# A decoder layer on one core: the expert stage's second bias as one float32r product of split rows

## The chip, the cores and the metric

The kernel runs on one core of one Trainium2 chip. Its time is the device time of one execution in microseconds (us). A core has TensorE (matrix products; loads of its stationary operand are listed apart), VectorE, ScalarE and GpSimd (in the rows: PE, PEld, DVE, ACT, POOL), and a queue for transfers on SyncE (SP). They run side by side, each through its own list of instructions, and wait for one another on semaphores. Products go into eight banks of PSUM, everything else on the core lies in SBUF.

## The reference, cut to what matters

A decoder layer for x of 16 x 128 x 256: self attention, cross attention, and a third block with an attention of its own and four experts. Only the last part is touched, on 2048 tokens with 4 experts and 256 hidden columns:

```python
raw = softmax(x @ w_gate)                    # 4 values for each token
top_vals, top_idx = top_k(raw, 2)
w = softmax(top_vals)
comb = zeros((t, 4)).at[arange(t)[:, None], top_idx].add(w)
hmid = gelu(einsum('td,edi->tei', x, we1) + be1[None])
eout = einsum('tei,eid->ted', hmid, we2) + be2[None]
out = einsum('te,ted->td', comb, eout)       # then h + out and a layer norm
```

The bias be2 enters as comb @ be2: for each token the sum of four rows of be2, each times its gate weight.

## The kernel before, in words

The program runs its stages one after another on each engine: A and B (the first two attentions), C (the third), D (the experts). The order of the work in each engine's list is written out by hand. Stage D takes the 2048 tokens as 16 blocks of 128, in four chunks c of four blocks b; experts are x = 0 to 3. Chunk 0's hidden layer is made at the end of stage C. Then for c = 1 to 3 a loop over m = 0 to 7 makes the hidden layer of chunk c (one half of one expert for each m) and, at each odd m, combines one block of chunk c-1. Chunk 3 is combined last, by itself.

float32 values are multiplied exactly enough by splitting them: a high part rounded to float32r, and a low part that is the value minus the high part. A product of split values is three products (high x high, high x low, low x high), and float32r products of 256 columns are one pass each. In stage D:

- hidden_pe (L2066) makes a half of an expert's hidden layer in six products (L2074 to L2076). hidden_act (L2254) applies gelu (L2263) and rounds to the high part D_HH (L2269), hidden_pool (L2302) subtracts to get the low part D_HL (L2305). xt_pe, xt_act, xt_low turn the normalized x of a later chunk and split it in the same way (L1621 is the subtraction).
- gate_pe (L2053) makes the gate's logits with 4 columns each (L2062); gate_dve, in three parts, makes the gate weights in some eighteen small instructions on VectorE (L2142 to L2183). The last writes 16 values for each token, 4 blocks x 4 experts, into the first 16 columns of D_comb, a 128x128 tile that is otherwise zero.
- comb_t_pe (L2079) transposes D_comb on TensorE (L2082), so that the weight of block b and expert x lies in row 4b+x, and comb_t_act (L2271) copies the 128x128 result from the bank to D_combT on ScalarE (L2275).
- TensorE's combine (L2093) makes, for each block, six products for each expert (L2115 to L2117) and one for the bias (L2109), ahead of expert 1's, or of expert 2's in the last chunk. The bias product has D_combT as stationary operand and one block of the table D_b2, 128x4x256, as moving one: rows 4b to 4b+3 of block b hold be2, the others are zero. Both are plain float32. An expert's bank is used again four turns later, when VectorE has read it.
- VectorE's combine (L2188) waits for the first expert's bank with the bias, adds the residual to the bias (L2196), adds the four experts times their gate weight one after another (L2202) and takes the statistics for the layer norm (L761 to L765). GpSimd raises the variance to the power -0.5 (L771), and VectorE's finish applies it to the block before (L776). In the last chunk ScalarE scales experts 0 and 1 (L2299), GpSimd sums them with the residual (L2341, L2344), and VectorE does the bias (L2214) and experts 2 and 3 (L2221).
- norm_step (L1565 to L1578) and norm_pool (L1584) normalize the blocks of a later chunk for its hidden layer; VectorE does two steps at each m below 4 in c = 1 and 2.
- SyncE loads the table once (L2366), when stage C is nearly over, and stores each block when it is done.
- The turns of banks 6, 7, 0 and 1 are shared by the hidden layer, the gate, x and the transposed weights; dtakes (L2012) notes for each turn what releases it.

Of the kernel before, what the change touches and what calls it, by code (L numbers as in the profile page):

```python
# [43 lines left out]
def program(nc, I, out):  # L44
# [1441 lines left out]
    comb = [T[:, 0:16].rearrange("p (a b) -> p a b", a=4) for T in comb128]  # L1486
    combT = [sb(f"D_combT{i}", [128, 128], F32, st_d) for i in range(2)]
    X2 = [sb(f"D_X2{i}", [128, 4, 256], F32, st_d) for i in range(2)]
    yD = [sb(f"D_y{i}", [128, 256], F32, st_d) for i in range(2)]
    tD = [sb(f"D_t{i}", [128, 2, 256], F32, st_d) for i in range(2)]  # L1490
    st_d.close()

# [538 lines left out]
    for c in range(1, NCH):  # L2031
        for m in range(8):
            if c + 1 < NCH and XT_FIRST <= m < XT_FIRST + 2:
                dtakes_xt(c + 5, m - XT_FIRST)
            dtakes_h(c, m)
            if m == 1:
                dtakes(("ct", c - 1), ("ct_act", c))
                dtakes(("gate", c), ("gate_dve", 18 * c + 1))

    dtakes(("ct", NCH - 1), ("ct_act", NCH))  # L2040

# [48 lines left out]
    def pe_d(e):  # L2090
        q = Queue(e, sem)

        def combine(c, b):  # L2093
            i = c % 2
            bs = slice(b * 128, b * 128 + 128)
            q.wait_ge("ld_b2", 16)
            for x in range(4):
# [9 lines left out]
                if x == CONSTANT[c]:  # L2107
                    q.wait_ge("ct_act", c + 1)
                    e.matmul(ebank(c, b, x)[:, 256:512], combT[i][:, :], b2[:, b, :], start=True, stop=True)  # L2109
                o = ebank(c, b, x)[:, 0:256]  # L2110
# [25 lines left out]
    def gate_dve(e, q, c, part):  # L2136
# [35 lines left out]
        if part == 2:  # L2172
            if c < 2:
                e.memset(comb128[c][:, :], 0.0).then_inc(sem("comb_zero"), 1)
            q.wait_ge("gate_act", 2 * c + 2)
            e.tensor_tensor(ew[:, :, :], ew[:, :, :], sel[:, :, :], ALU.mult).then_inc(sem("gate_dve"), 1)
            q.wait_ge("gate_dve", n + 15)
            e.tensor_reduce(mx[:, :], ew[:, :, :], AX.X, ALU.add).then_inc(sem("gate_dve"), 1)
            q.wait_ge("gate_dve", n + 16)
            e.reciprocal(mx[:, :], mx[:, :]).then_inc(sem("gate_dve"), 1)  # L2180
            q.wait_ge("gate_dve", n + 17)
            q.wait_ge("comb_zero", min(c, 1) + 1)
            e.tensor_tensor(comb[c % 2][:, :, :], ew[:, :, :], bc(mx[:, :]), ALU.mult).then_inc(sem("gate_dve"), 1)  # L2183

    def dve_d(e):
# [43 lines left out]
        for c in range(1, NCH):  # L2229
            for m in range(8):  # L2230
                if c + 1 < NCH and m < 4:
                    norm_step(e, q, c + 5, 2 * m)
                    norm_step(e, q, c + 5, 2 * m + 1)
                if m % 2:
                    j = 4 * (c - 1) + m // 2
                    combine(c - 1, m // 2)
                    if j:
                        finish(j - 1)
                    if m < 7:
                        gate_dve(e, q, c, m // 2)  # L2240
        for b in range(4):
            combine_last(b)
# [28 lines left out]
    def comb_t_act(e, q, c):  # L2271
        q.wait_ge("ct_pe", c + 1)
        if c >= 2:
            q.wait_ge("od_pe", 16 * (c - 1))
        e.activation(combT[c % 2][:, :], dbank(("ct", c))[:, 0:128], ACT.Copy).then_inc(sem("ct_act"), 1)  # L2275

    def act_d(e):
        q = Queue(e, sem)

        for c in range(1, NCH):  # L2280
            for m in range(8):
                if c + 1 < NCH and XT_FIRST <= m < XT_FIRST + 2:
                    xt_act(e, q, c + 5, m - XT_FIRST, dbank(("xt", c + 5, m - XT_FIRST)))
                    xh_act(e, q, c + 5, m - XT_FIRST)
                if m == 1:
                    comb_t_act(e, q, c - 1)
                hidden_act(e, q, c, m)
# [172 lines left out]
def layouts(a):  # L2460
# [34 lines left out]
    for b in range(4):  # L2495
        f["Db2"][4 * b:4 * b + 4, b, :] = g("be2").reshape(4, 256)
    f["x"] = np.asarray(a["x"])
# [18 lines left out]
```

## Time and profile before

| | |
|---|---|
| time of the kernel, median of 3 runs | 1184.74 us (1183.73 to 1185.34) |
| time of the profiled execution | 1184.21 us |
| its span in the profile | 1182.4 us |
| TensorE busy | 1113.7 us, 94% |
| loads of its stationary operand | 920.0 us, 78% |
| VectorE busy | 954.8 us, 81% |
| ScalarE busy | 669.1 us, 57% |
| GpSimd busy | 661.2 us, 56% |
| stage D on its own | about 1080 to 1182 us |

The span is the time from the first to the last instruction of the profiled execution; the execution's own time has 1.8 us more. Times in the trace count from the span's start. A busy share is an average over stages with different limits, and TensorE's ends are modelled, so that a share near 100% doesn't mean that it is at its peak. A row of the timeline gives the start, the duration, the engine, the line, the operation, what is written from what, its shape, how many instructions are merged into the row, and, in brackets, how long the engine had been idle before and what ended that. Matmul durations overlap: the distance of their starts is what each takes up.

### The profile page before, as it was taken

What the parts mean: (1) busy time and instruction counts of PE and PEld (TensorE: products, weight loads), DVE (VectorE), ACT (ScalarE), POOL (GpSimd) and SP (SyncE); (2) the same over time, 40 slices, a digit from 0 to 9 for tenths busy, and PEclk for the clock granted to TensorE, in tenths of its full rate; (3) what the DMA queues carried; (4) which work ended last, traced back from release to release, by engine and by line L of the source; (5) the groups of instructions that cost most, each with busy time, mean ns of one, the idle gap of its engine ahead of it and who ended that gap; (6) DMA issues with size and microseconds to landing.
All of it is one profiled execution on the core that took longest, in us unless ns stands there. A gap on an engine that the chain in (4) does not pass through costs nothing.

```text
span 1182.4 us, 30629 instructions
## 1 busy us (share of the span) xinstructions
PE 1113.7 (94%) x11732; PEld 920.0 (78%) x11732; DVE 954.8 (81%) x2219; ACT 669.1 (57%) x1703; POOL 661.2 (56%) x714
## 2 busy tenths in 40 slices
PE   6899999799999999888999999999999999999997
PEld 5667666566666766556899899999999899988887
DVE  6768877887878878867788888888888888868977
ACT  5466564577777777564555444444444444558663
POOL 4467564645555555264778554444544455737665
PEclk9899999999999999989999999999999999999999
DMA  5875544354444444302111000000000100101111
GB/s 160 212 185 132 128 125 112 97 138 123 126 121 131 119 126 126 104 21 89 61 66 55 1 1 1 1 1 1 1 1 1 37 2 1 37 19 36 37 37 36
DMA packets 107491, 83.05 MB, mean 70 GB/s; under 512 B 74172, under 2 KB 95804, under 8 KB 107346
## 3 DMA queue, kind: packets, MB, share of 16 engines
q1 hardware_dynamic: 107345, 81.10, 24.6%
q8 instruction: 93, 1.52, 0.5%
q14 instruction: 53, 0.43, 0.1%
HBM read 57.02 MB, written 23.07 MB: 68 GB/s over the span
## 4 chain that ended last, share of the span: by engine, by line
PE 56%; DVE 14%; issue 6%; POOL 4%; ACT 2%; SPq 1%; DMA 0%; POOLq 0%; DVEq 0%; ACTq 0%
PE bank L1632 5%; PE bank L1633 5%; PE bank L1634 5%; PE bank L1688 4%; PE bank L1661 4%; PE bank L663 4%; PE bank L641 3%; PE bank L560 3%; DVE B_nr L803 2%; PE bank L1648 2%; PE bank L1703 2%; PE bank L1701 2%; PE bank L1702 2%; PE bank L1649 2%; PE bank L1650 2%
## 5 line engine op out<-in xcount | busy, mean ns | idle before, releaser
L1936 POOL TENSOR_TENSOR C_QK<-C_t1b,C_t2b 128x512 f32<-128x512 f32 x128 | 168.8, 1319 | 227.2 <-DVE C_t2b L1775 226.6
L1772 DVE SCALAR_TENSOR_TENSOR C_t1b<-bank,C_bcol,C_tabs 64x512 f32<-64x512 f32 x256 | 192.0, 750 | 38.4 <-PE bank L1634 34.3
L803 DVE TENSOR_REDUCE B_nr<-bank 128x4 f32<-128x512 f32 x256 | 164.3, 684 | 24.3 <-PE bank L602 23.8
L1062 ACT ACTIVATE PT<-bank 128x512 f32<-128x512 f32 x224 | 130.1, 596 | 92.4 <-PE bank L641 90.8
L1632 PE MATMUL bank<-C_XTh,C_Wh 128*128 128x512 f32 x256 | 112.4, 439 | 5.7 <-DVE C_XTl L1621 1.9
L1868 ACT ACTIVATE C_P<-bank,C_nm 128x128 f32<-128x128 f32 x256 | 90.7, 367 | 34.2 <-DVE C_nm L1785 32.6
L1887 ACT ACTIVATE C_V<-bank 128x512 f32<-128x512 f32 x64 | 38.1, 597 | 124.1 <-PE bank L1650 122.5
L1633 PE MATMUL bank<-C_XTl,C_Wh 128*128 128x512 f32 x256 | 101.7, 397 | 0.0
L1634 PE MATMUL bank<-C_XTh,C_Wl 128*128 128x512 f32 x256 | 101.2, 395 | 0.0
L663 PE MATMUL bank<-PT,vpool 128*32 128x128 f32 x2048 | 97.1, 285 | 2.0 <-ACT OTf L1072 2.0
L1775 DVE SCALAR_TENSOR_TENSOR C_t2b<-bank,C_bcol,C_tabs 128x512 f32<-128x512 f32 x128 | 96.1, 751 | 1.8
L641 PEld LDWEIGHTS bank<-stk 54*128 54x128 bf16 (+1 forms) x1280 | 49.2, 96 | 48.6 <-issue 36.8
L1876 ACT ACTIVATE C_OTh<-bank,C_bcol 128x512 fp32r<-128x512 f32 x64 | 44.1, 690 | 73.3 <-PE bank L1688 72.8
L602 PE MATMUL bank<-stk 48*128 48x128 bf16 (+1 forms) x1280 | 76.2, 218 | 4.1 <-DVE B_nr L803 3.7
L1796 DVE SCALAR_TENSOR_TENSOR C_OTl<-bank,C_bcol,C_OTh 128x512 fp32r<-128x512 f32 x64 | 47.9, 749 | 38.8 <-ACT C_OTh L1876 38.7
L641 PE MATMUL bank<-stk 54*128 54x128 bf16 (+1 forms) x1280 | 76.7, 221 | 2.5 <-DMA stk<-A_nmT 2.3
L1648 PE MATMUL bank<-C_Wh,C_XTh 128*128 128x256 f32 x256 | 72.5, 283 | 1.6 <-DVE C_t2b L1775 1.2
L1701 PE MATMUL bank<-C_Wh,C_OTh 128*128 128x256 f32 x256 | 71.9, 281 | 0.4 <-DVE C_OTl L1796 0.4
L1649 PE MATMUL bank<-C_Wl,C_XTh 128*128 128x256 f32 x256 | 71.9, 281 | 0.0
L1650 PE MATMUL bank<-C_Wh,C_XTl 128*128 128x256 f32 x256 | 71.8, 280 | 0.0
L1703 PE MATMUL bank<-C_Wh,C_OTl 128*128 128x256 f32 x256 | 71.7, 280 | 0.0
L1702 PE MATMUL bank<-C_Wl,C_OTh 128*128 128x256 f32 x256 | 71.6, 279 | 0.0
(271 smaller groups left out, 3495.8 us busy)
## 6 DMA issues: line engine op xcount, KB each, us to landing
Adrq<-PB SPq DMA_DIRECT2D x16, 192.0 KB, 3.0
Adrk<-PB SPq DMA_DIRECT2D x16, 192.0 KB, 3.2
stk<-Adrq SPq DMA_DIRECT2D x16, 192.0 KB
stk<-Adrk SPq DMA_DIRECT2D x16, 192.0 KB
Bdrq<-PB SPq DMA_DIRECT2D x16, 192.0 KB, 3.0
stk<-Bdrq SPq DMA_DIRECT2D x32, 96.0 KB
Bdrk<-PB SPq DMA_DIRECT2D x16, 192.0 KB, 2.8
stk<-Bdrk SPq DMA_DIRECT2D x32, 96.0 KB
```

The costliest lines, as they stand in the source:

```text
L641: m = e.matmul(bank2(n)[:, j * 128:j * 128 + 128], (AS if kd else KS[L])[i3][rows, h, :], QS[L][i3][rows, h, :], start=alone, stop=alone o ...
L663: m = e.matmul(o[32 * j:32 * j + 32, c3 * 128:c3 * 128 + 128], vp[:, h, :], pt_of(n)[:, j * 128:j * 128 + 128], start=first or not L, stop ...
L803: e.tensor_reduce(dst, bank[n % 2][:, :].rearrange("p (a b) -> p a b", a=4), AX.X, ALU.max, negate=True).then_inc(sem("m_dve"), 1)
L1062: e.activation(pt_of(n)[:, :], bank2(n)[:, :], ACT.Exp).then_inc(sem("e_act"), 1)
L1632: e.matmul(o[:, :], CWh[hp][:, cs], XCh[0][:, t, :], start=t == 0, stop=False)
L1633: e.matmul(o[:, :], CWh[hp][:, cs], XCl[0][:, t, :], start=False, stop=False)
L1634: m = e.matmul(o[:, :], CWl[hp][:, cs], XCh[0][:, t, :], start=False, stop=t == 1)
L1648: e.matmul(ob, XCh[0][:, t, xs], CWh[hp][:, cs], start=t == 0, stop=False)
L1649: e.matmul(ob, XCh[0][:, t, xs], CWl[hp][:, cs], start=False, stop=False)
L1772: e.scalar_tensor_tensor(out=v4(t1b[kq][lo:lo + 64, :]), in0=v4(o[hi:hi + 64, :]), scalar=bc[hi:hi + 64, :], in1=tabsC[hi:hi + 64, 2 * kq ...
L1775: e.scalar_tensor_tensor(out=v4(t2b[kq][:, :]), in0=v4(o[:, :]), scalar=bc, in1=tabsC[:, 2 * kq, :].unsqueeze(1).to_broadcast([128, 4, 128 ...
L1936: e.tensor_tensor(QK[v % 3][:, kq, :], t1b[kq][:, :], t2b[kq][:, :], ALU.add).then_inc(sem("rc_pool"), 1)
```

## The change

The bias product becomes one float32r product, made exact by three sets of rows 32 apart. The gate weights are written three times, in columns 0, 32 and 64 of D_comb. After the transpose, D_combT (now float32r) holds the rounded weights in rows 0, 32 and 64, and in rows 32 to 63 a subtraction on VectorE puts the low part in their place. The table is loaded with be2 in three sets of rows as well, rounded as a whole by a copy on ScalarE into a new tile D_b2r, and its rows 64 to 95 are replaced by their low part by VectorE. So one product sums high x high, low x high and high x low.

comb_t_dve is called at m = 1 of each c, ahead of VectorE's combine, and before the last chunk; bias_act and bias_dve run once, at c = 1 and m = 1. The semaphore ct_act becomes ct_low and counts two for each chunk, and combine waits for ld_b2 of 18 instead of 16.

```diff
-    combT = [sb(f"D_combT{i}", [128, 128], F32, st_d) for i in range(2)]
+    combT = [sb(f"D_combT{i}", [128, 128], F32R, st_d) for i in range(2)]
+    b2r = sb("D_b2r", [128, 4, 256], F32R, st_d)
...
-                dtakes(("ct", c - 1), ("ct_act", c))
+                dtakes(("ct", c - 1), ("ct_low", 2 * c))
...
         def combine(c, b):
...
-            q.wait_ge("ld_b2", 16)
+            q.wait_ge("ld_b2", 18)
...
                 if x == CONSTANT[c]:
-                    q.wait_ge("ct_act", c + 1)
-                    e.matmul(ebank(c, b, x)[:, 256:512], combT[i][:, :], b2[:, b, :], start=True, stop=True)
+                    q.wait_ge("ct_low", 2 * c + 2)
+                    e.matmul(ebank(c, b, x)[:, 256:512], combT[i][:, :], b2r[:, b, :], start=True, stop=True)
...
-            e.tensor_tensor(comb[c % 2][:, :, :], ew[:, :, :], bc(mx[:, :]), ALU.mult).then_inc(sem("gate_dve"), 1)
+            e.tensor_tensor(comb128[c % 2][:, 0:96].rearrange("p (k r) -> p k r", k=3)[:, :, 0:16].rearrange("p k (a b) -> p k a b", a=4),
+                            ew[:, :, :].unsqueeze(1).to_broadcast([128, 3, 4, 4]),
+                            mx[:, :].unsqueeze(1).unsqueeze(3).to_broadcast([128, 3, 4, 4]), ALU.mult).then_inc(sem("gate_dve"), 1)
...
+                if m == 1:
+                    if c == 1:
+                        bias_dve(e, q)
+                    comb_t_dve(e, q, c - 1)
                 if m % 2:
                     j = 4 * (c - 1) + m // 2
                     combine(c - 1, m // 2)
...
+        comb_t_dve(e, q, NCH - 1)
         for b in range(4):
             combine_last(b)
...
-        e.activation(combT[c % 2][:, :], dbank(("ct", c))[:, 0:128], ACT.Copy).then_inc(sem("ct_act"), 1)
+        e.activation(combT[c % 2][:, :], dbank(("ct", c))[:, 0:128], ACT.Copy).then_inc(sem("ct_low"), 1)
+
+    def comb_t_dve(e, q, c):
+        low = slice(32, 64)
+        q.wait_ge("ct_low", 2 * c + 1)
+        e.tensor_tensor(combT[c % 2][low, :], dbank(("ct", c))[low, 0:128], combT[c % 2][low, :].bitcast(F32),
+                        ALU.subtract).then_inc(sem("ct_low"), 1)
+
+    def bias_act(e, q):
+        q.wait_ge("ld_b2", 16)
+        q.wait_ge("xc_dve", 16)
+        e.activation(b2r[:, :, :], b2[:, :, :], ACT.Copy).then_inc(sem("ld_b2"), 1)
+
+    def bias_dve(e, q):
+        low = slice(64, 96)
+        q.wait_ge("ld_b2", 17)
+        e.tensor_tensor(b2r[low, :, :], b2[low, :, :], b2r[low, :, :].bitcast(F32), ALU.subtract).then_inc(sem("ld_b2"), 1)
...
                 if m == 1:
+                    if c == 1:
+                        bias_act(e, q)
                     comb_t_act(e, q, c - 1)
...
     for b in range(4):
-        f["Db2"][4 * b:4 * b + 4, b, :] = g("be2").reshape(4, 256)
+        for k in range(3):
+            f["Db2"][32 * k + 4 * b:32 * k + 4 * b + 4, b, :] = g("be2").reshape(4, 256)
```

## Rows read from the trace of the kernel before

**Rows 1.** Windows of the stage: us; busy time of each engine; TensorE's granted clock; transfers.

```profile
1090.00:1100.00 10.00, 10.00 (x71) 9.32 (x71) 9.45 (x17) 9.00 (x12) 7.56 (x7) 1.00 0.04 13
...
1140.00:1150.00 10.00, 10.00 (x70) 9.30 (x69) 5.27 (x15) 4.88 (x8) 7.98 (x9) 1.00 0.27 80
```

**Rows 2.** Waits from 1080 us on: total us, times, longest.

```profile
DVE D_y L2196 <- PE bank L2117: 5.9, 3, 2.7
```

**Rows 3.** Timeline, the table's load and the first block of chunk 0.

```profile
1045.94 0.33 SPq L2366 DMA_DIRECT2D D_b<-in_Db  x1
...
1082.11 0.37 PE L2115 MATMUL bank<-C_Wh,D_HH 128*128 128x256 f32 x1
...
1082.89 0.26 ACT L2275 ACTIVATE D_combT<-bank 128x128 f32<-128x128 f32 x1
...
1083.13 0.70 DVE L1570 TENSOR_SCALAR ve<-mv 128x4 f32<-128x4 f32 x1
1083.20 0.30 PEld L2109 LDWEIGHTS bank<-D_b,D_combT 128*128 128x128 f32 x2 [0.34 <-ACT D_combT L2275]
...
1083.76 1.30 POOL L2305 TENSOR_TENSOR D_HL<-D_G,D_HH 128x512 fp32r<-128x512 f32 x1
...
1084.33 0.29 PE L2117 MATMUL bank<-C_Wh,D_HL 128*128 128x256 f32 x1
...
1084.75 0.43 DVE L2196 TENSOR_TENSOR D_y<-bank,D_X 128x256 f32<-128x256 f32 x1 [0.93 <-PE bank L2117]
```

**Rows 4.** Single lines of the whole span: duration ns least/median/most, first and last start, forms.

```profile
L1850 ACT ACTIVATE C_Wh<-C_z x8: 1051/1052/1056, 562.6 to 1017.9; 128x1024 fp32r<-128x1024 f32 x8
...
L784 DVE TENSOR_TENSOR B_Wl<-vpool,B_Wh x2: 1226/1284/1343, 69.6 to 86.8; 128x1024 fp32r<-128x1024 f32 x2
...
L843 DVE TENSOR_TENSOR stk<-bank,rr x32: 214/286/358, 239.7 to 544.1; 128x192 f32<-128x192 f32 x16, 128x64 f32<-128x64 f32 x16
...
L2161 DVE TENSOR_TENSOR D_equal<-D_equal,D_lower x4: 1199/1212/1219, 1073.9 to 1154.8; 128x64 f32<-128x64 f32 x4
```

**Rows 5.** Timeline of TensorE around a bias product of the last chunk.

```profile
1164.20 0.28 PE L2117 MATMUL bank<-C_Wh,D_HL 128*128 128x256 f32 x1
...
1164.87 0.28 PE L2116 MATMUL bank<-C_Wl,D_HH 128*128 128x256 f32 x1
```

**Rows 6.** Timeline, the first block combined in c = 2.

```profile
1110.98 0.60 PE L2109 MATMUL bank<-D_b,D_combT 128*128 128x256 f32 x2
...
1112.33 0.21 DVE L1570 TENSOR_SCALAR ve<-mv 128x4 f32<-128x4 f32 x1
...
1112.51 0.42 DVE L2196 TENSOR_TENSOR D_y<-bank,D_X 128x256 f32<-128x256 f32 x1
```

**Rows 7.** Timeline, the first two blocks combined in c = 3.

```profile
1135.38 0.50 PE L2074 MATMUL bank<-D_XTh,C_Wh 128*128 128x512 f32 x1 [0.94 <-POOL D_XTl L1621]
...
1138.60 0.28 ACT L2275 ACTIVATE D_combT<-bank 128x128 f32<-128x128 f32 x1 [0.16 <-PE bank L2082]
...
1138.70 0.40 DVE L776 TENSOR_SCALAR X<-D_y,mv,rstd 128x256 f32<-128x256 f32 x1
...
1140.01 0.59 PE L2109 MATMUL bank<-D_b,D_combT 128*128 128x256 f32 x2
...
1148.44 0.42 DVE L2196 TENSOR_TENSOR D_y<-bank,D_X 128x256 f32<-128x256 f32 x1 [2.67 <-PE bank L2117]
```

**Rows 8.** Timeline of VectorE between chunk 2's last block and chunk 3's first.

```profile
1165.21 0.41 DVE L776 TENSOR_SCALAR X<-D_y,mv,rstd 128x256 f32<-128x256 f32 x1
1168.42 0.43 DVE L2214 TENSOR_TENSOR D_y<-bank,D_t 128x256 f32<-128x256 f32 x1 [2.81 <-POOL D_t L2344]
```

**Rows 9.** Windows, columns as in rows 1.

```profile
500.00:502.00 2.00, 2.00 (x32) 0.84 (x26) 1.93 (x6) 0.44 (x1) 0.00 (x0) 0.50 0.14 55
...
1176.00:1178.00 2.00, 0.23 (x2) 0.02 (x1) 1.79 (x6) 0.00 (x0) 0.65 (x1) 1.00 0.19 66
...
1180.00:1181.00 1.00, 0.00 (x0) 0.00 (x0) 0.28 (x1) 0.00 (x0) 0.00 (x0) 0.55 0.39 131
```

More of the change, by code:

```diff
@@ L2036, in program @@
             if m == 1:
-                dtakes(("ct", c - 1), ("ct_act", c))
+                dtakes(("ct", c - 1), ("ct_low", 2 * c))
                 dtakes(("gate", c), ("gate_dve", 18 * c + 1))
-    dtakes(("ct", NCH - 1), ("ct_act", NCH))
+    dtakes(("ct", NCH - 1), ("ct_low", 2 * NCH))
     def dbank(key):
```

## The prediction

> **What bounds the kernel now.** I read the page's busy shares first (the table above) and then the windows of the last stage, the only one that the change touches. In 1090 to 1100 us TensorE is recorded as 100% busy and VectorE as 94%, so busy time doesn't say which sets the pace; in 1140 to 1150 VectorE falls to 53% under the same full TensorE [rows 1]. The waits decide: from 1080 us to the end VectorE waits for a product only three times, 5.9 us in all [rows 2]. The first is 0.93 us at 1084.75 [rows 3], the last 2.67 us at 1148.44 [rows 7], so one of 2.3 us lies between. Listed in order of time, VectorE has no other gap from 1084.75 to 1139.1, and TensorE's restart at 1135.38 is released by GpSimd's low rows, which queue behind a power that waits for VectorE [rows 7]. So the stage runs in stretches: VectorE sets the pace from about 1083 to 1134, TensorE from 1135.38 to 1148.44, VectorE again to 1165.6; then GpSimd's sums hold VectorE for 2.81 us, until 1168.42 [rows 8], and from there VectorE runs to the end with gaps of hundredths.
>
> **Part 1: the cheaper product.** A bias product is two passes. From the product before it (1164.20) to the second product behind it (1164.87) is 0.67 us, where neighbours without a bias product lie 0.12 apart, 0.24 for the two steps [rows 5]: it costs 0.43. As one float32r product of the same 256 columns it costs 0.12 like its neighbours. It gives back 0.31, 16 times, 5.0 us of TensorE. Only products on the path count. In the TensorE stretch there are two, at 1140.01 and 1147.0; the first is shown [rows 7]. Term: -0.6. The four of the last chunk don't count: VectorE has no gap behind 1168.42.
>
> **Part 2: the bias table.** bias_act and bias_dve come at the worst place, the start of the stage. ScalarE reaches comb_t_act at 1082.89 [rows 3]; a copy of 128x1024 goes ahead of it. Such copies took 1.05 us [rows 4], so it ends at 1083.94; the load that it also waits for was issued 37 us earlier [rows 3]. The two instructions of hidden_act behind it slip by 1.05 us; they open chunk 1's next buffer, which combine of chunk 0 doesn't read. On VectorE bias_dve is ready behind ve at 1083.83 [rows 3] and may start at 1084.0. A subtraction with 1024 elements in each partition took 1.23 us at its shortest [rows 4]; that this one has 32 partitions I price at nothing. But GpSimd's L2305 runs from 1083.76 to 1085.06 [rows 3], and a VectorE instruction with two SBUF inputs has shown what that means: L2161, 64 elements, took 1.21 us each of four times [rows 4], while L843 with a PSUM input took 0.21 for 64 elements and 0.36 for 192 [rows 4]. I take the long case: bias_dve ends at 1085.06 + 1.23 = 1086.3. Free of GpSimd it would be 1085.2.
>
> The Trainium skill, "SBUF — State Buffer", section "SBUF: two separate sides", has the rule: a VectorE instruction with two SBUF inputs and a GpSimd one exclude each other for the whole instruction, whichever started first. By it the end is 1086.3, without it 1085.2; the traces above bear it out.
>
> Behind it comes comb_t_dve on 32x128 from PSUM, 0.29 between those two, to 1086.6. Now TensorE: combine waits for ld_b2 of 18 ahead of its **first** product, not of the bias product. The six products of expert 0 started at 1082.11 [rows 3]; now they start at 1086.35. From there to the last product of expert 1 it took 2.22 us (1082.11 to 1084.33), of which 0.34 was the wait for the copy [rows 3] and 0.31 falls away: last start at 1087.92. With its 0.29 and the 0.13 that lay between its end and VectorE's start (1084.62 to 1084.75), L2196 comes at 1088.3 instead of 1084.75. Term: +3.5; with no waiting for GpSimd +2.5. Since VectorE has no gap for the next 50 us, nothing takes it back: TensorE, GpSimd and ScalarE move along with it.
>
> **Part 3: the clock.** TensorE now stops from 1082.1 to 1086.35, 4.2 us. At the end of the program its work is over 0.23 us behind 1176, and the granted clock is 1.00 until then and 0.55 in 1180 to 1181 [rows 9], so it went to the lower level, 1.2 GHz, at about 1180.1, 3.9 us after the work. A stop of 4.2 us should do the same, and in 500 to 502 us it was down for the whole window with TensorE busy throughout [rows 9], so work alone doesn't lift it at once. The 13 products between the restart and L2196 then lie 0.23 instead of 0.12 apart, +1.4; those of experts 2 and 3 behind them can add up to 1.1 more, since VectorE takes 0.5 us for each expert. I take +1.5, bounds 0 and +2.5.
>
> The Trainium skill, "TensorE: Matmul & The Clock Gate", section "What's actually happening", says that the slow state is the default and activity releases it. By that rule the change costs 6.1 us, without it 4.6.
>
> **Part 4: comb_t_dve in later chunks.** It stands in VectorE's queue ahead of combine, and the bias product waits for it. In chunk 2 TensorE was at its bias product at 1110.98 while VectorE was still in norm steps until 1112.54 [rows 6]. Both come later by the same amount, so the gap stays: comb_t_dve ends at 1112.83, the bias product starts at 1112.9, six products and the latency as above give L2196 at 1114.05 instead of 1112.51. VectorE had been behind TensorE and is now in a round trip with it. Term: +1.5, no less than +1.3. In chunk 3 VectorE is idle from 1139.1, ScalarE's copy is done at 1138.88 and the bias product comes at 1140.01 [rows 7], so it is covered; without that cover it would be 1.5 again. For the last chunk it stands behind finish, which ends at 1165.62 [rows 8], so TensorE stops from 1164.3, a step behind 1164.20 [rows 5], to 1165.95. VectorE waits for GpSimd until 1168.42 anyway; TensorE restarts 1.4 us late and wins 0.3 with each of three more bias products, so ScalarE's scaled copies and GpSimd's sums come late by 1.4, 1.1 and 0.8 into gaps of about that size. I put 0.1 there, bounds 0 and 0.4.
>
> **Part 5: the rest.** The gate weights go from 16 to 48 written elements; by the slope of L843 [rows 4] that is 0.04 each, 0.1 on the path. Bank turns released later by comb_t_dve are next used four turns on. The table is the same 512 KB, on no queue that moves.
>
> **The sum.** 3.5 + 1.5 + 1.5 - 0.6 + 0.1 + 0.1 = +6.1 us. The profiled execution took 1184.21 us (span 1182.4, 1.8 around it) and would take 1190.3; the median shown is 0.5 higher, so I forecast 1190.8, 0.5% slower. No change can be told within 0.2%, 2.4 us.
>
> **The rivals.** (a) The clock holds, or bias_dve isn't held by GpSimd: +3.3 to +5.0, 1188.0 to 1189.7. For it: TensorE had shorter stops, 0.94 us at 1135.38 [rows 7], at full clock; against it: this stop is longer than the 3.9 us. (b) It costs more, +7.5 to +10, 1192.2 to 1194.7: the slow level outlasts combine, or it falls again in chunk 2, where TensorE stops for 1.9 us. (c) The preparation is covered: if VectorE took back the lost time in its waits of 5.0 us at 1141 and 1148, only part 4 would be left, +1.0, 1185.7. Against it: those waits are set by TensorE's start at 1135.38, which itself follows VectorE [rows 7] and moves along. (d) Faster: if TensorE set the pace of the whole stage, as its 100% in [rows 1] would have it, each of the 16 products gives 0.31, 5.0 us, 1179.7. It decides where VectorE reaches comb_t_dve before TensorE reaches the bias product; it does so in chunk 3 alone, and at the start TensorE would have to wait less than 0.3 us for the table where I count 4.2.
>
> **How the numbers follow.** Forecast (+5.0 to +7.5) 0.50; (a) 0.27; (b) 0.10; (c) 0.08; (d) 0.05. All of the forecast, (a) but for its lowest part and the lower half of (b) give a range of 1187.8 to 1193.2, some 0.8. Faster 0.04, within 0.2% 0.09 (nearly all of c, a little of d), slower 0.87.
>
> **What would show it.** VectorE's idle time ahead of L2196 in the first chunk near 3.5 us or more instead of 0.93; bias_dve recorded at 2.2 us rather than 1.2; a stop of 4 us in TensorE at 1082 with a granted clock of 0.5 behind it; a new VectorE wait of over 1 us near 1114 plus the shift; L2109 with 16 instructions of 0.28; the wait at 1148 shorter by 0.6. It is wrong if VectorE's stretches aren't shifted as a whole, or if GpSimd's contention with it falls out differently: each of L1578's and the gate's small instructions moves by up to 1 us with that.

## The result and the profile after

The changed kernel took 1192.49 us (median of 6 runs, 1187.56 to 1194.25), the kernel before 1184.24 us beside it (6 runs, 1181.42 to 1186.41). The ratio is 1.0066, 95% interval [1.0043, 1.0089]: slower, by 8.25 us between the medians. The time lies inside the range that was given, but 1.7 us above the number forecast, at the place where rival (b) began (1192.2).

The profiled execution took 1189.57 us, its span is 1187.7 us. All engines' totals together say little of what happened; this is the busy row of the page after:

```profile
PE 1104.5 (93%) x11716; PEld 913.2 (77%) x11716; DVE 960.0 (81%) x2224; ACT 668.7 (56%) x1704; POOL 661.6 (56%) x714
```

TensorE has 9.2 us less to do than before and the kernel is slower: its sum was not what counted. The 16 products fewer are the second passes.

**One measure for all runs.** The stages ahead of stage D scatter by some us between executions, so I count from an instruction that every kernel but e9's has at the same place, the start of the last small step of the norm ahead of chunk 0's combine (`ve`, L1570 before, L1571 after), to the end of the span. Before: 1182.4 - 1083.13 [rows 3] = 99.27 us. After: 1187.7 - 1082.02 = 105.68. The difference, **+6.41 us**, is what stage D lost in this execution, and I call it the loss of stage D. In the same way the lateness of an instruction is how much later after `ve` it starts than its counterpart before. Of the kernel before there is one profile, and every loss is counted against it; e4 and e11, two profiles of one kernel, differ by 0.02 us by this measure. In e9 a subtraction moves ahead of `ve` and delays `ve` itself, so for e9 I count from the last reduction of the gate ahead of it as well.

**The start.** Timeline of the changed kernel, chosen engines' rows:

```profile
1081.75 1.04 ACT L2294 ACTIVATE D_b2r<-D_b 128x1024 fp32r<-128x1024 f32 x1
1082.02 0.64 DVE L1571 TENSOR_SCALAR ve<-mv 128x4 f32<-128x4 f32 x1
1082.59 1.26 POOL L2331 TENSOR_TENSOR D_HL<-D_G,D_HH 128x512 fp32r<-128x512 f32 x1
...
1082.82 2.11 DVE L2299 TENSOR_TENSOR D_b2r<-D_b,D_b2r 32x1024 fp32r<-32x1024 f32 x1 [0.16 <-ACT D_b2r L2294]
1083.82 1.71 POOL L2342 TENSOR_TENSOR D_X<-D_X,X 128x256 f32<-128x256 f32 x1
1084.97 0.28 DVE L2288 TENSOR_TENSOR D_combT<-bank,D_combT 32x128 fp32r<-32x128 f32 x1
1084.99 0.58 PE L2116 MATMUL bank<-C_Wh,D_HH 128*128 128x256 f32 x1 [3.88 <-DVE D_b2r L2299]
1086.44 0.41 PE L2110 MATMUL bank<-D_b2r,D_combT 128*128 128x256 f32 x1
1086.65 0.41 PE L2116 MATMUL bank<-C_Wh,D_HH 128*128 128x256 f32 x1
1088.22 0.42 DVE L2199 TENSOR_TENSOR D_y<-bank,D_X 128x256 f32<-128x256 f32 x1 [2.97 <-PE bank L2118]
```

VectorE's subtraction takes 2.11 us and lies over GpSimd's L2331, as in the long case of Part 2. TensorE stops for 3.88 us and then the products start 0.21 us apart (1086.44, 1086.65), where they lay 0.12 apart before [rows 5]. The add comes 6.20 us behind `ve`, before 1.62 [rows 3]: lateness 4.58. In the windows the granted clock shows the lower level, 1.2 GHz, for most of 1084 to 1088 us, and full level in chunk 1 and in the last chunk (columns as in [rows 1]):

```profile
1084.00:1088.00 4.00, 3.01 (x14) 3.01 (x15) 1.22 (x2) 0.19 (x1) 3.74 (x3) 0.57 0.01 4
1116.00:1120.00 4.00, 3.55 (x29) 3.54 (x30) 2.35 (x6) 0.00 (x0) 2.86 (x3) 1.00 0.30 105
...
1174.00:1180.00 6.00, 6.00 (x52) 6.00 (x51) 5.43 (x15) 1.86 (x5) 4.17 (x6) 1.00 0.08 28
```

**The waits from 1080 us on**, total, times and longest:

```profile
DVE D_y L2199 <- PE bank L2118: 8.4, 4, 3.0
...
PE bank L2116 <- DVE D_b2r L2299: 3.9, 1, 3.9
PE bank L2110 <- DVE D_combT L2288: 3.8, 2, 1.9
DVE D_y L2217 <- POOL D_t L2370: 2.5, 1, 2.5
```

Against [rows 2] VectorE's wait for a product has a fourth case. The two stops of TensorE behind comb_t_dve are those of chunk 1 and of the last chunk. Chunk 1, then two neighbouring products and the second waiting block of the TensorE stretch, then the last chunk, from the timeline:

```profile
1116.02 0.28 DVE L2288 TENSOR_TENSOR D_combT<-bank,D_combT 32x128 fp32r<-32x128 f32 x1
1116.45 0.36 PE L2110 MATMUL bank<-D_b2r,D_combT 128*128 128x256 f32 x1 [1.83 <-DVE D_combT L2288]
1117.65 0.43 DVE L2199 TENSOR_TENSOR D_y<-bank,D_X 128x256 f32<-128x256 f32 x1 [1.35 <-PE bank L2118]
...
1145.25 0.28 PE L2110 MATMUL bank<-D_b2r,D_combT 128*128 128x256 f32 x1
1145.37 0.28 PE L2116 MATMUL bank<-C_Wh,D_HH 128*128 128x256 f32 x1
...
1153.07 0.42 DVE L2199 TENSOR_TENSOR D_y<-bank,D_X 128x256 f32<-128x256 f32 x1 [2.36 <-PE bank L2118]
...
1168.96 0.48 DVE L2205 SCALAR_TENSOR_TENSOR D_y<-bank,D_comb,D_y 128x256 f32<-128x256 f32 x1 [0.46 <-DVE D_y L2205]
1170.22 0.40 DVE L776 TENSOR_SCALAR X<-D_y,mv,rstd 128x256 f32<-128x256 f32 x1
1170.66 0.28 DVE L2288 TENSOR_TENSOR D_combT<-bank,D_combT 32x128 fp32r<-32x128 f32 x1
1171.09 0.36 PE L2110 MATMUL bank<-D_b2r,D_combT 128*128 128x256 f32 x1 [1.94 <-DVE D_combT L2288]
1173.44 0.42 DVE L2217 TENSOR_TENSOR D_y<-bank,D_t 128x256 f32<-128x256 f32 x1 [2.49 <-POOL D_t L2370]
```

What I call chunk 1 is combined in the loop's turn c = 2; the prediction's Part 4 and its rival (b) call it chunk 2. The lateness of these: chunk 1's add 35.63 behind `ve` against 29.38 [rows 6], 6.25; the add at 1153.07 is 71.05 against 65.31 [rows 7], 5.74; L776 at 1170.22 is 88.20 against 82.08 [rows 8], 6.12; the first sum at 1173.44 is 91.42 against 85.29 [rows 8], 6.13; the end 6.41. So the loss is paid at the start (4.58) and in chunk 1 (1.67 at its first add), 0.5 less is left behind the TensorE stretch, and 0.67 is added from there to the end, 0.38 of it ahead of L776, mostly in the gap of 0.46 at 1168.96.

The median difference of 8.25 us is larger than the 6.41 of this one execution. That difference was the open question for the runs.

### The profile page after: what moved, and what is told of

It reads as the page before. It is cut to its first block, busy times and chain, and to the rows that moved or that the text cites. A ratio compares the mean times of both kernels' runs of the same rounds, so it can differ in the third digit from the quotient of the medians.

```text
span 1187.7 us, 30604 instructions
## 1 busy us (share of the span) xinstructions
PE 1104.5 (93%) x11716; PEld 913.2 (77%) x11716; DVE 960.0 (81%) x2224; ACT 668.7 (56%) x1704; POOL 661.6 (56%) x714
## 4 chain that ended last, share of the span: by engine, by line
PE 55%; DVE 13%; issue 7%; POOL 4%; ACT 2%; SPq 1%; DMA 0%; POOLq 0%; DVEq 0%; ACTq 0%
PE bank L1633 5%; PE bank L1634 5%; PE bank L1635 4%; PE bank L1689 4%; PE bank L1662 4%; PE bank L663 3%; DVE B_nr L803 2%; PE bank L641 2%; PE bank L560 2%; PE bank L1649 2%; PE bank L1704 2%; PE bank L1702 2%; PE bank L1703 2%; PE bank L1650 2%; PE bank L1651 2%
```

## The experiments

In the table, "loss" is that of stage D in the profiled execution against the kernel before, and "lateness" that of VectorE's add in chunk 0's first block and in chunk 1's first, in the same execution. The row of e9 is by `ve`; counted from the gate its loss is -0.12.

| run | median, before beside it | ratio [95%] | loss | lateness: first, chunk 1 |
|---|---|---|---|---|
| changed kernel | 1192.49, 1184.24 | 1.0066 [1.0043, 1.0089] | +6.41 | 4.58, 6.25 |
| e4, changed kernel again | 1194.05, 1184.90 | 1.0067 [1.0048, 1.0085] | +7.92 | 4.63, 6.87 |
| e11, and again | 1194.92, 1184.83 | 1.0075 [1.0047, 1.0103] | +7.90 | 4.63, 6.85 |
| e1, table prepared earlier | 1188.17, 1184.90 | 1.0023 [1.0010, 1.0035] | +3.33 | 0.66, 3.11 |
| e2, chunk 1's comb_t_dve earlier | 1191.05, 1184.90 | 1.0049 [1.0030, 1.0068] | +6.13 | 4.63, 6.06 |
| e3, TensorE kept busy at the start | 1190.09, 1184.90 | 1.0036 [1.0020, 1.0051] | +5.32 | 3.36, 5.06 |
| e10, kept busy at all three stops | 1189.94, 1184.83 | 1.0044 [1.0029, 1.0059] | +5.14 | 3.38, 5.03 |
| e5, table awaited at the bias product | 1192.64, 1184.47 | 1.0064 [1.0049, 1.0079] | +9.11 | 3.74, 6.32 |
| e6, cheap product alone | 1183.74, 1184.47 | 0.9993 [0.9975, 1.0011] | -1.01 | -0.30, -0.33 |
| e7, before, bias product twice | 1188.85, 1184.47 | 1.0030 [1.0014, 1.0046] | +3.13 | 0.45, 1.49 |
| e8, all preparations earlier | 1185.98, 1184.47 | 1.0014 [1.0003, 1.0025] | +2.07 | 1.21, 2.28 |
| e9, placed again | 1183.17, 1184.83 | 0.9987 [0.9975, 1.0000] | -0.61 | -1.19, -0.30 |

**e1: the table prepared in the last step of the stage before.** The copy and the subtraction move from chunk 1's m = 1 to the end of the attention stage; the copy's wait on all of `xc_dve` becomes three waits on the buffers' last users.

```diff
@@ dve_c
+            if u == NU - 1:
+                bias_dve(e, q)
@@ act_c
+            if u == NU - 1:
+                bias_act(e, q)
...
-        q.wait_ge("xc_dve", 16)
+        q.wait_ge("rc_pool", 2 * NU)
+        q.wait_ge("xb_c_pool", 16)
+        q.wait_ge("oc_pe", NU - 2)
```

> The changed kernel with bias_act and bias_dve moved into gaps of stage C (ScalarE behind the turn of the last unit, VectorE behind its reciprocal), some 20 us ahead of their use; nothing is left out. My theory, that the start of stage D costs 4.6 us because TensorE waits for the table and comes back at the lower clock: no stop of 3.9 us at the start and no granted clock of 0.5 there; VectorE's first L2199 is late only by comb_t_dve, +0.7 us against before; the whole stage is 3.9 us shorter than in the changed kernel, total +2.5 us against before. Rival 1, the preparation costs the same wherever it stands, since stage C has no room: +4.8 us or more, with the longer waits in stage C. Rival 2, the loss isn't the table but the thrice written weights and the subtraction of the weights: +5.5 to +6.5 us, L2199 still late by over 3 us.

The first add is late by 0.66 instead of 4.58, so 3.9 us of the start were the table with its clock. The loss is +3.33, where 2.5 was expected: 3.1 less than the changed kernel's, so 0.8 of what was won went in chunk 1 and the last chunk. Rival 1 is out (the median, too, is only 3.3 us over that of before), and so is rival 2. There comb_t_dve still makes TensorE stop, and here the lower clock followed, as it had not in the changed kernel's first profile. Chunk 1's rows and, behind them, the windows of chunk 1 and of the last chunk:

```profile
1115.39 0.42 DVE L2203 TENSOR_TENSOR D_y<-bank,D_X 128x256 f32<-128x256 f32 x1 [2.11 <-PE bank L2122]
...
1113.42 0.55 PE L2114 MATMUL bank<-D_b2r,D_combT 128*128 128x256 f32 x1 [1.83 <-DVE D_combT L2290]
```

```profile
1112.00:1116.00 4.00, 2.58 (x12) 2.61 (x13) 1.73 (x7) 0.00 (x0) 3.82 (x4) 0.60 0.38 131
1167.00:1171.00 4.00, 3.65 (x18) 3.68 (x19) 1.37 (x4) 0.00 (x0) 2.42 (x4) 0.57 0.11 37
```

The same stop of 1.83 us as after, but VectorE waits 2.11 us instead of 1.35 behind it. By chunk 1's last block, though, the lateness is down from 3.11 to 1.78, for a reason given under e4. In the last chunk the lateness went from 1.13 at the end of the TensorE stretch to 3.34 at the end of the program, 2.2 us, where the changed kernel's went up by 0.67 at full clock.

**e2: chunk 1's comb_t_dve ahead of the norm steps.**

```diff
             for m in range(8):
+                if c == 2 and m == 0:
+                    comb_t_dve(e, q, c - 1)
```

> The changed kernel with comb_t_dve of chunk 1 (called in c = 2) moved ahead of the norm steps in VectorE's queue, where ScalarE's copy is just done; nothing is left out. My theory, that chunk 1 costs 1.7 us because TensorE's bias product waits for VectorE to get through its norm steps and VectorE then for TensorE: the wait of 1.35 us ahead of L2199 in that chunk and TensorE's stop of 1.8 us disappear, 1.4 us less than the changed kernel, +5.0 us against before. Rival 1, the 1.7 us are the subtraction's own time and contention with GpSimd: no change beyond 0.3 us. Rival 2, VectorE only waits elsewhere (for ScalarE's copy): at most 0.5 us less.

VectorE has no wait ahead of chunk 1's first add any more:

```profile
1118.82 0.49 DVE L1571 TENSOR_SCALAR ve<-mv 128x4 f32<-128x4 f32 x1
1119.34 0.42 DVE L2199 TENSOR_TENSOR D_y<-bank,D_X 128x256 f32<-128x256 f32 x1
```

Lateness rises only from 5.28 (chunk 0's last block) to 6.06 instead of from 4.58 to 6.25: 0.8 instead of 1.7. Of the 0.8, 0.44 is comb_t_dve with its spacing, and 0.34 comes at `ve`: 0.52 us from its start to the add, against 0.18 in [rows 6]. The round trip of Part 4 is real, and rival 1 (no change beyond 0.3) doesn't hold for this stretch. The loss as a whole is +6.13, not the +5.0 expected, because the low clock at the start lasted longer here (the lateness went from 4.63 to 5.39 within chunk 0, and was 5.28 at its last block). The stop of the last chunk was 1.94 us here, and the clock stayed full behind it.

**e3: TensorE kept busy while it waits for the table.** 28 products more, into a bank that is overwritten later, stand ahead of the first combine; nothing else is changed.

```diff
+                if m == 1 and c == 1:
+                    q.wait_ge("xc_dve", 16)
+                    q.wait_ge("hl_pool", 1)
+                    for _ in range(28):
+                        e.matmul(ebank(0, 0, 3)[:, 0:256], HH[0][:, 0, 0:128], CWh[1][:, 0:256], start=True, stop=True)
```

> The changed kernel with 28 extra products of 256 columns on TensorE in its stop at the start of stage D (their result is overwritten); they take 3.3 us at full clock, less than the stop of 3.9 us. My theory, that the lower clock behind the stop costs VectorE 1.1 us: the granted clock stays at 1.00 at the start of stage D, the products behind the stop lie 0.12 instead of 0.21 us apart, and the first L2199 comes 1.0 us earlier; total 1.1 us less than the changed kernel, +5.3 us against before. Rival, the clock hurts nothing because VectorE's own work hides it: same as the changed kernel, +6.4 us. If the extra products outlast the wait for the table, it is slower by what they outlast it.

The stop shrinks to 0.47 us, the clock is full behind it, and the products are 0.12 apart:

```profile
1088.00:1092.00 4.00, 3.53 (x29) 3.33 (x28) 2.27 (x3) 0.76 (x2) 4.00 (x4) 1.00 0.00 0
```

```profile
1089.63 0.39 PE L2116 MATMUL bank<-C_Wh,D_HH 128*128 128x256 f32 x1 [0.47 <-DVE D_b2r L2304]
...
1090.45 0.28 PE L2110 MATMUL bank<-D_b2r,D_combT 128*128 128x256 f32 x1
1090.57 0.28 PE L2116 MATMUL bank<-C_Wh,D_HH 128*128 128x256 f32 x1
1091.59 0.42 DVE L2204 TENSOR_TENSOR D_y<-bank,D_X 128x256 f32<-128x256 f32 x1 [1.70 <-PE bank L2118]
```

The first add is late by 3.36 instead of 4.58. So 3.4 us are the table and 1.2 us the clock, against 3.5 and 1.5 in the prediction, and the loss is +5.32 for 5.3 expected.

**e4 and e11: the changed kernel again**, to see how one execution stands to another. No edit.

> The changed kernel as it is, profiled again beside the others. My theory: from the norm step that ends at 1082.2 us (L1571) to the end of the span 105.7 us within 0.7, against 99.3 in the kernel before, with the same stops; what its six runs differ by (1187.6 to 1194.3 us) lies ahead of stage D. Rival: stage D itself varies by over 1.5 us, because the clock falls a second time (chunk 1 or the last chunk) in some executions; then the length of stage D differs and a second stretch of 0.5 is seen.

> The changed kernel once more, for a third profile. My theory: the stop at the start brings the lower clock every time, those in chunk 1 and in the last chunk in some executions only, for 1.5 us more in the last chunk each time it falls there; stage D 6.3 to 8.5 us longer than before. Rival, that one of the two profiles so far was an exception: always 6.4, without a lower clock behind the first block.

Both start like the first profile (4.63 against 4.58), and then lose 7.92 and 7.90 us. The windows of e4 behind the start, in chunk 1 and in the last chunk:

```profile
1088.00:1092.00 4.00, 4.00 (x20) 4.00 (x20) 1.07 (x3) 0.00 (x0) 2.33 (x3) 0.50 0.02 4
1120.00:1124.00 4.00, 4.00 (x25) 4.00 (x23) 2.53 (x6) 0.00 (x0) 1.83 (x2) 0.57 0.07 26
1174.00:1178.00 4.00, 4.00 (x23) 4.00 (x23) 1.82 (x4) 0.48 (x1) 1.91 (x4) 0.58 0.11 37
```

In the same three places e11's windows of 4 us have 0.50, 0.63 and 0.57.

The low clock came in all three profiles at the start, and in two of three in chunk 1 and in the last chunk. In e4 the lateness rises in chunk 1 from 5.05 to 6.87, and in the last chunk from 5.68 at the end of the TensorE stretch to 7.90, 2.2 us. So my theory for e4, a stage D that doesn't vary, is wrong, and its rival came; e11's expectation held.

**What the low clock in chunk 1 cost: nothing by the end of the chunk.** At chunk 1's last block the lateness is 6.37 in the changed kernel's first profile, 6.33 in e4 and 6.37 in e11. What is lost at the chunk's first add comes back right behind it, at the four instructions of VectorE that normalize a later chunk (L1579). The changed kernel's first profile, then e4:

```profile
1121.90 4.29 DVE L1579 TENSOR_SCALAR C_XN<-X,mv,rstd 128x256 f32<-128x256 f32 x4
...
1125.41 1.81 DVE L1579 TENSOR_SCALAR C_XN<-X,mv,rstd 128x256 f32<-128x256 f32 x4
```

In the first profile GpSimd works from 1121.85 to 1126.03 almost without a gap, and each of the four takes 0.83 to 1.48 us. In e4 GpSimd waits 1.09 us for ScalarE, until 1127.19, and three of the four take 0.40 us. The row takes 4.2 to 4.3 us in all profiles with the full clock in chunk 1, 1.8 in e4, e11 and e5, and 2.8 in e1. So the 1.5 us that e4 and e11 lose beyond the first profile are those of the last chunk. Only in e5, where the low clock of chunk 1 lasted longer, was more lost than came back. That the slower TensorE is what keeps GpSimd waiting is read from these profiles and not tested by a run of its own.

**e10: all three stops kept busy.** e3 with 12 products more ahead of the first bias product of chunk 1 and of the last chunk.

```diff
                 if x == CONSTANT[c]:
+                    if b == 0 and c in (1, 3):
+                        for _ in range(12):
+                            e.matmul(ebank(c, b, x)[:, 256:512], HH[i][:, 0, bs], CWh[1][:, 0:256], start=True, stop=True)
```

> The changed kernel with extra products on TensorE in all three stops (28 at the start, 12 at the bias product of chunk 1 and 12 at that of the last chunk, each shorter than its stop; their result is overwritten). My theory, that what the changed kernel's executions differ by is whether the clock falls at the three stops: no granted clock of 0.5 in stage D, its length 5.2 us over that of before in the profile, and the median 5 to 5.5 us over before instead of 8 to 9. Rival, that the surplus of the median lies ahead of stage D: median still 7 us or more over before.

```profile
1086.00:1092.00 6.00, 5.51 (x44) 5.20 (x43) 3.96 (x8) 0.47 (x1) 4.09 (x4) 1.00 0.00 0
1116.00:1124.00 8.00, 7.68 (x54) 6.95 (x53) 6.12 (x20) 1.61 (x3) 5.57 (x7) 1.00 0.28 84
1170.00:1178.00 8.00, 7.58 (x63) 7.38 (x62) 5.06 (x15) 1.76 (x4) 5.55 (x8) 1.00 0.05 17
```

The clock is full at all three places, the loss is +5.14, and now the medians differ by about the same, 5.11 us. Beside it on the same chip the changed kernel (e11) lost 7.90 in its profile and 10.09 between medians, 1.0075 of 1184.83 being 8.9. A kernel with 52 useless products is thus 3 to 5 us faster than the changed one: that much of the typical time is the clock. The intervals of the two ratios, [1.0029, 1.0059] and [1.0047, 1.0103], overlap, so the size rests on the profiles (2.76 us). Of these 1.25 are at the first add (4.63 against 3.38) and 1.55 in the last chunk (a rise of 2.2 against 0.6); at chunk 1's last block the two differ by what they differed by at the start.

**e5: the wait for the table at the bias product, not at the first product.**

```diff
-            q.wait_ge("ld_b2", 18)
             for x in range(4):
...
                 if x == CONSTANT[c]:
+                    q.wait_ge("ld_b2", 18)
```

> The changed kernel with the wait for the finished table (ld_b2 of 18) moved from the start of combine to the bias product; nothing is left out. My theory: the six products of expert 0 run at once, at the start of the stage, and only the bias product and what follows wait until bias_dve and comb_t_dve are through; TensorE restarts 0.3 us later (behind comb_t_dve) with 7 products instead of 13 ahead of L2199, at the lower clock 0.21 us apart: L2199 comes 3.4 to 3.9 us late instead of 4.6, total 0.7 to 1.2 us less than the changed kernel when the clock falls as often. Rival, that where the wait stands doesn't matter because VectorE sets the pace: no change.

```profile
1086.91 0.55 PE L2110 MATMUL bank<-D_b2r,D_combT 128*128 128x256 f32 x1 [3.47 <-DVE D_combT L2288]
```

```profile
1086.00:1092.00 6.00, 5.09 (x25) 5.12 (x25) 3.23 (x8) 0.00 (x0) 3.25 (x3) 0.50 0.01 3
```

Six products are done ahead of the stop and the first add is late by 3.74 instead of 4.58. But the clock was low through the whole window, and chunk 1 too was slow (6.32 to 7.71 within it): the loss was the largest of all profiles, +9.11, and the ratio is that of the changed kernel. The 0.7 to 1.2 us expected did not come; whether the low clock lasted longer because of the edit or by chance, one profile can't show. The rival, no change, has the median right, though the first add did come earlier.

**e6: the cheap product without what it needs.** The table is copied early as in e1, the low rows of table and weights are left out: no subtraction, weights written once, comb_t_dve gone. So the bias is that of one rounding only.

```diff
-                    q.wait_ge("ct_low", 2 * c + 2)
+                    q.wait_ge("ct_low", c + 1)
...
-                    comb_t_dve(e, q, c - 1)
...
-        comb_t_dve(e, q, NCH - 1)
```

> The cheaper product alone: table copied to float32r in stage C, and both subtractions, the thrice written weights and their waits left out, so the weights and the table are only rounded and the low parts missing from the result. My theory, that 16 cheaper products give only what lies where TensorE sets the pace: L2199 of the first chunk 0.3 us earlier, of the last TensorE stretch 0.6 more, at most 1.2 us faster than before in stage D. Rival, that TensorE is the stage's bound: 5.0 us faster.

The loss is -1.01 us and the ratio 0.9993 [0.9975, 1.0011]. Lateness is -0.30 at the first add, -0.33 in chunk 1, -0.99 at the end of the TensorE stretch and at the end. That is one product at the start (0.31) and two in the TensorE stretch (0.66): three of 16 count. Rival (d), 5.0 us, is out, also as an upper limit of what this idea can give with all its preparations free.

**e7: the kernel before with each bias product done twice**, so that its cost on the path shows with the other sign.

```diff
-                    e.matmul(ebank(c, b, x)[:, 256:512], combT[i][:, :], b2[:, b, :], start=True, stop=True)
+                    for _ in range(2):
+                        e.matmul(ebank(c, b, x)[:, 256:512], combT[i][:, :], b2[:, b, :], start=True, stop=True)
```

> The kernel before with every bias product made twice (the second overwrites the first), 0.43 us more on TensorE 16 times; the output is the same. My theory, that VectorE sets the pace: 0.4 at the start, 0.9 in the TensorE stretch, some of the four in the last chunk, +1.3 to +2.2 us. Rival, that TensorE is the stage's bound: +6.9 us.

```profile
DVE D_y L2197 <- PE bank L2118: 8.2, 4, 3.1
...
DVE D_y L2215 <- PE bank L2118: 0.7, 1, 0.7
```

The loss is +3.13, ratio 1.0030 [1.0014, 1.0046]: above the 1.3 to 2.2 expected and less than half of 16 x 0.43 = 6.9. The start (0.45) and the TensorE stretch (0.93, two products) are as counted. Chunk 1 (1.04, a new wait of 0.93) and the last block (0.67, a wait of 0.72) are new: there TensorE's slack is smaller than 4 x 0.43 = 1.7 us. The off-path products are hidden only up to that.

**e8 and e9: the same work in other places.** e8 is e1 and e2 together, with ScalarE's copy of chunk 0's weights ahead of hidden_act and the last comb_t_dve ahead of finish. e9 moves two of them further: chunk 0's comb_t_dve between the norm steps, the last one into the combine of block 11.

```diff
+                if j == 11 and x == 1:
+                    comb_t_dve(e, q, NCH - 1)
...
+                if c == 1 and m == 1:
+                    comb_t_dve(e, q, 0)
```

> The changed kernel with all its new parts moved to where their engine is free: table in stage C, the first copy of the transposed weights ahead of the hidden layer on ScalarE, comb_t_dve of chunk 1 ahead of the norm steps, that of the last chunk between the statistics and finish; nothing is left out. My theory: L2199 of the first chunk 0.3 to 0.7 us earlier than before, +0.3 for the subtraction in chunk 1, -0.6 in the TensorE stretch, and in the last chunk TensorE still stops for over 1 us, so that the clock may fall there: -0.5 us where it holds, +1.0 where it falls, the median within 0.2% of the kernel before. Rival, that the three sets of rows cost by themselves: +2 us or more.

> The version with moved parts, and two of them moved once more: comb_t_dve of chunk 0 between VectorE's norm steps, as soon as ScalarE's copy is there, and that of the last chunk inside VectorE's combine of the block before, behind expert 1; nothing is left out. My theory, that only stops of TensorE and VectorE's own 0.28 us matter: no stop at any bias product, no granted clock of 0.5 in stage D, first L2199 0.6 us earlier than before, +0.3 in chunk 1, -0.6 in the TensorE stretch, +0.3 to +0.7 in the last chunk: -0.6 to 0.0 us against before in stage D. Rival, that a version with these instructions can't get below +1 us because they lie on VectorE's path wherever they stand: +1.3 us or more.

In e8 the first add was to come 0.3 to 0.7 us earlier than before and came 1.21 later, since comb_t_dve still stood behind `ve`: TensorE stopped for 1.10 us at the start, and the clock went down behind it:

```profile
1082.98 0.39 PE L2114 MATMUL bank<-D_b2r,D_combT 128*128 128x256 f32 x1 [1.10 <-DVE D_combT L2294]
```

```profile
1083.00:1087.00 4.00, 4.00 (x22) 4.00 (x22) 1.87 (x4) 0.35 (x1) 3.72 (x4) 0.57 0.01 4
```

e9 has no such stop and no low clock in stage D ahead of the end of TensorE's work. Window and VectorE rows of its start:

```profile
1080.00:1083.00 3.00, 3.00 (x25) 2.98 (x26) 2.54 (x11) 2.86 (x6) 2.26 (x3) 1.00 0.00 0
```

```profile
1081.01 0.28 DVE L2296 TENSOR_TENSOR D_combT<-bank,D_combT 32x128 fp32r<-32x128 f32 x1
...
1082.97 0.43 DVE L2203 TENSOR_TENSOR D_y<-bank,D_X 128x256 f32<-128x256 f32 x1 [0.22 <-PE bank L2122]
```

The loss is +2.07 in e8 and -0.61 in e9 by `ve`, where the changed kernel has +6.4 to +7.9. But in e9 comb_t_dve stands ahead of `ve` (1081.01 against 1082.54) and makes it late. From the gate's last reduction (D_mx<-D_ew, 1080.36 before, 1079.28 in e9) to the end of the span it is 102.04 us before and 101.92 in e9, a loss of -0.12, and the first add is early by 0.70 and not by 1.19; for all other runs the two ways of counting agree within 0.04. The +2.07 of e8 is what its rival said (the three sets of rows cost by themselves, 2 us or more); e9, with the same rows, rules that out. e9 has all the arithmetic of the change and a ratio of 0.9987 [0.9975, 1.0000], at the edge of what can be told from no change: the best of all versions that compute everything, 1.7 us below before between the medians, of which its profile shows 0.1 in stage D; where the rest comes from isn't shown.

## Why the prediction was right, and where it fell short

**What bounds the kernel: right.** VectorE sets the pace but for the TensorE stretch; e6 shows that the cheaper product counts three times of 16 (-1.0 us), and the changed kernel's first profile took back nothing of the start in the 50 us behind it. One reading was off: VectorE does not run from 1168.42 to the end with gaps of hundredths, it waits 0.44 us for GpSimd at 1179.86. Every profile has that wait, so it changes nothing in the sum.

**Part 1: right.** The float32r bias product starts 0.12 ahead of its neighbour (1145.25, 1145.37). The term of -0.6 can be read between chunk 1 and the second waiting block: lateness from 6.37 at chunk 1's last block to 5.74, with the wait at 2.36 instead of 2.67 [rows 7].

**Part 2: right.** The subtraction took 2.11 us, counted as 2.2 by the long case, and TensorE's stop was 3.88 us, counted as 4.2. e3 gives 3.4 for the term of 3.5. That an instruction of VectorE with two SBUF inputs takes 2.11 us where 1.23 was the shortest [rows 4] is what the Trainium skill, "SBUF — State Buffer", section "SBUF: two separate sides", describes as exclusion for a whole instruction; the trace agrees, for an instruction on 32 partitions too. e1 shows the other order: the same subtraction, started at 1061.72 and so 0.05 us ahead of GpSimd's L1949, took 1.22 us, and that one 2.07, where the others of its line took 1.03 to 1.04.

**Part 3: right in kind, 1.2 us for 1.5 at the first add, and too narrow in place.** The low clock behind the stop is in every profile that has a stop of over 3 us (changed kernel three times, e2, e5). Its price at the first add is 4.58 - 3.36 = 1.2 us. But it lasted longer than the first block in some: lateness rose within chunk 0 by another 0.4 to 1.0 us (e4 4.63 to 5.05, e2 4.63 to 5.39, e5 3.74 to 4.73), which I had only as the upper bound of +2.5. In e4 and e11 this was given back by chunk 1's last block.

**Part 4, chunk 1: right, 1.67 for 1.5** (6.25 - 4.58), with a wait of 1.35 us as said. It held for the full clock. With the low clock it is 1.8 to 2.5 at the first add (e4: 6.87 - 5.05; e1: 3.11 - 0.66), but over the whole chunk 1.4 and 1.1 (e4: 6.33 - 4.95; e1: 1.78 - 0.66), less than the 1.8 at full clock (6.37 - 4.58), since the four L1579 are then free of GpSimd; only in e5, where the low clock lasted longest, it is 3.0 (7.61 - 4.62). The prediction named these instructions' dependence on GpSimd as a sign of being wrong and put no price on it.

**Part 4, the last chunk: the term that was mis-sized.** I put 0.1 there, bounds 0 and 0.4, since a GpSimd wait of 2.8 us would cover TensorE's stop. Measured: 0.67 in the first profile at full clock, 2.2 in e4, e11 (5.72 to 7.92) and e1, where the clock went down. Two things were missing. The gap of 0.46 us of VectorE ahead of the fourth scaled add of block 11 (1168.96) stands in front of comb_t_dve and makes the stop 1.94 us instead of 1.65. In e9, which has neither this stop nor the gap, the rise is 0.3. And I asked whether the clock would fall in chunk 1 (rival (b)), but never for the last chunk, where a stop of the same kind comes: half speed takes TensorE's lead there, and ScalarE's and GpSimd's parts come late behind it.

**The sum.** 6.1 forecast, 6.41 in the first profile, 7.9 in the two others. The closeness of the first is in part luck: the start cost 4.58 where the sum has 5.0, and the last chunk 0.67 where it has 0.1. The forecast case was the one of the first profile, rival (b) that of the others and of the medians by its number: ratios of 1.0066, 1.0067 and 1.0075 are 7.8, 7.9 and 8.9 us. I gave (b) 0.10, since the shorter stop in [rows 7], 0.94 us, had kept the full clock; of stops of 1.1 to 1.9 us the trace of before showed nothing, and that was no ground for holding them harmless. Both places that (b) names did see the low clock in e4 and e11 (behind the first block, and in chunk 1), yet they were paid back by chunk 1's last block; what made these profiles longer is the last chunk, which (b) doesn't name. e10 separates the parts: 5.1 us without any low clock, the rest is clock.

**The rivals.** (a) did not come (the low clock is at the start of every profile). (c) did not: the table's 4.58 us went through to the end. (d) is excluded by e6.

**What stays open.** The gap of 0.46 us in block 11 is in all three profiles of the changed kernel and in e1, e2, e3, e5, e8 and e10, 0.46 or 0.47 us each time, and is not in e6, e7, e9 or before. Its row names the instruction ahead of it on the same engine as what ended it, and no semaphore; what VectorE does in it isn't shown. e9 both moves comb_t_dve into that place and loses the gap, which doesn't settle it. Also open is why the same stop of 1.8 us brings the low clock in one execution and not in the next. In the profiles of e4 and e11 the low clock at the start had lasted longer than in the first one; whether that matters isn't shown, since e2 has it as well and kept the full clock behind 1.94 us, and e1, with the full clock at the start, saw the low one in chunk 1 and in the last chunk. In e9 the lateness rises by 0.79 in chunk 1, as it does in e2 and e8, in the same two places.

## What to carry to other kernels

Before an engine's cheaper instruction is worth its preparation, count how many of those instructions stand ahead of a wait that ends last; here it was 3 of 16, 1.0 us, and the preparation cost 7 to 9 (the loss of 6.4 to 7.9 and the 1.0 won). Preparations belong where their engine has time and the consumer has none waiting: the same instructions moved by a few microseconds took the loss from +6.4 to -0.1. And a new stop of TensorE isn't only its own length: look at every place where one of a microsecond or more is added, and price half the clock behind it, also where the stop itself seems covered. Then follow it to the end of the stage: in chunk 1 the lower clock moved GpSimd's work out of VectorE's way, and the price was gone a block later; in the last chunk it stayed.

## What the runs showed of the hardware

The granted clock went to the lower level behind stops of TensorE as short as 1.10 us (e8) and 1.83 us (e1), in chunk 1 in two of three profiles of the same kernel, while it stayed full behind 0.94 us [rows 7] in before, 1.12 us at 1083.94 in e1, 1.26 us at 1140.62 in the changed kernel, 1.57 us at 1129.93 in e9 and 1.94 us at 1172.67 in e2. So here the length of the stop alone didn't decide it. I had counted on a stop of about 3.9 us for it. The Trainium skill, "TensorE: Matmul & The Clock Gate", section "What's actually happening", has the slow state as the default that activity releases. e4 agrees in kind: TensorE was busy throughout 1088 to 1092 us at 0.50, and the granted clock was 0.81 in the two microseconds behind and 1.00 from 1094.

The exclusion between VectorE and GpSimd hit GpSimd as well: L2342 took 1.71 us at 1083.82, where the subtraction runs from 1082.82 to 1084.93, and 0.72 us at 1081.91.
